# Attention's last group and the first quantised layer: halves, score banks and the causal corner

## The chip, the cores and the metric

The kernel runs on one NeuronCore of a Trainium2 chip. The metric is the device time of one execution, in microseconds (us). The core has five engines with queues of their own: TensorE (PE in the profile, its weight loads PEld), VectorE (DVE), ScalarE (ACT), GpSimd (POOL) and SyncE (SP, which issues the DMAs here). They meet at semaphores only.

## The reference, cut to what matters

A batch of 16 sequences of 1024 rows and 256 channels goes through four residual layers: causal attention with 16 heads of 16 channels, a linear layer on values quantised to a 6-bit grid in blocks of 32, a Mamba block followed by an MLP, and the quantised layer again.

```python
x = x + _L0_attn_a_ref(_layernorm(x, axis=-1), L0_attn_a_Wqkv, L0_attn_a_Wproj)
x = x + _L0_ffn_ref(_layernorm(x, axis=-1), L0_ffn_weight, L0_ffn_bias)
x = x + _L0_attn_b_ref(_layernorm(x, axis=-1), ...)      # Mamba, then MLP
x = x + _L0_ffn_ref(_layernorm(x, axis=-1), L0_ffn_weight, L0_ffn_bias)
...
# in attention
scores = jnp.where(causal, scores, jnp.finfo(scores.dtype).min)
attn = jax.nn.softmax(scores, axis=-1)
y = jnp.einsum('bhqk,bhkd->bhqd', attn, V)
...
# in the quantised layer
scales = jnp.maximum(jnp.max(jnp.abs(blocks), axis=-1) / FP6_E2M3_MAX, eps)
q = _nearest_on_grid(blocks / scales[..., None], _GRID)
```

## The kernel before

A loop (`nc.Fori`, line 1317) makes 16 passes, one for each sequence, each about 655 us. In a pass each engine works through its own program (`sync_program`, `pool_program`, `scalar_program`, `vector_program`, `tensor_program`). The order of work on an engine is written out by hand. Rows stand on the 128 partitions, in 8 tiles of 128 rows; a half is 4 tiles (512 rows), a pair is 2.

**Attention** runs on one unit counter `u` that all engines' programs share. The 16 heads form 4 groups of 4. For each group come 48 S units: one score product for the row maxima (PE lines 1108, 1111 with the mask), reduced by DVE (line 836). One group and 14 units later come the group's 48 T units: a transposed score product (line 1132; on the diagonal a second product adds `mask2`, line 1135), whose exponential ACT writes to `PT` (line 619). Four T units (the four heads) form a step: one tile of 128 keys against up to 512 queries. The widths of the steps of a group are 512, 384, 256, 128 (first half of queries, all on the diagonal) and 512 x 4, 512, 384, 256, 128 (second half, the last four on the diagonal); steps count from 0 to 47 over the pass. Each step has four value products (line 1145), one step behind the exponentials (`pv_at`), summed in bank 6 until the half's last step. Then ACT evacuates bank 6 (line 626), PE transposes into bank 7 (line 1156), and DVE divides into `Y` (lines 859, 860). A T product waits until the exponential that used its PSUM bank is done: three banks, and from T unit 132 (`T6`), behind the last S unit, six.

**Behind attention** DVE's program runs in this order: `add_tiles(0, U)` adds the projected rows (line 793) and collects statistics (726, 732, 734); `quant_half(0, 0, th)` for the two halves normalises (738) and rounds to the grid (lines 240 to 262, two pairs side by side); `add_tiles(1, X)`; `layer_norm(1, th)` for both halves; `rms_rows(0, th)` for both (826). GpSimd computes the reciprocal roots (511, 517, 518), adds the bias (522) and multiplies the scales back (527). PE turns pairs of tiles (`turn`, line 1070), ACT evacuates them to `XNT` (601), PE multiplies tile by tile (`rows`, line 1087, two banks of rotation or more). Behind that the Mamba block starts with in-projections (PE line 1168, ACT line 647).

Of the kernel before, what the change touches and what calls it, by code (L numbers as in the profile page):

```python
# [76 lines left out]
def build(nc, x_in, wqkv_in, wproj_in, ipw_in, convw_in, convb_in, xpw_in, dtw_in, dtb_in, alog_in, d_in, opw_in,  # L77
          w1_in, w2_in, fw_in, fb_in, ident_in, mask_in, sel_in, cos_in, sin_in, ones_in, out):
    with ExitStack() as ctx:
# [17 lines left out]
        mask2 = sb("mask2", [P, P], BF16)  # L97
# [39 lines left out]
        PT = view(20480, 4096).rearrange("p (s t) -> p s t", s=2 * HG)  # L137
# [126 lines left out]
        with nc.Block() as block:  # L264
# [15 lines left out]
            def _(dve):  # L280
# [4 lines left out]
                nc.vector.tensor_copy(mask2[:, :], mst[:, 1, :])  # L285
# [18 lines left out]
            def _(pe):  # L304
                pe.wait_ge(pre["pool"], 1)

                for i in range(2):
# [22 lines left out]
        pv_at = [STEP_AT + HG * (s + 1) for s in range(NST * NG)]  # L330
# [49 lines left out]
        def row_bank(stage, i):  # L380

            return i % MB if stage == 2 else i % (2 * MB)
# [123 lines left out]
        def pool_program(pool):  # L506
# [13 lines left out]
            def quantized(f, k, th):  # L520
# [3 lines left out]
                  .then_inc(S("xb"), 1)  # L524
                for p in range(th * NT // 4, (th + 1) * NT // 4):
# [44 lines left out]
            quantized(1, 2, 0)  # L570
            layer_power(2, 1)
            quantized(1, 2, 1)
# [20 lines left out]
        def scalar_program(act):  # L593
            own = Chain(act, S("act_own"))

            def evacuate(rnd, pairs=range(NT // 2)):

                for p in pairs:
                    n = rnd * (NT // 2) + p
                    act.wait_ge(S("te_ready"), n + 1)  # L600
                    A(XNT[:, :, 2 * P * p:2 * P * (p + 1)], bank(6 + n % 2).rearrange("p (c t) -> p c t", c=NC),  # L601
# [10 lines left out]
            for u in range(U_END):  # L612
                n = u - NS1 - LAG
                if 0 <= n < NS2 * NG:
                    s, hh, g, qc, j, q0, w = t_unit(n)
                    act.wait_ge(S("ST"), n + 1)
                    if s >= 2:
                        act.wait_ge(S("PV"), s - 1)
                    A(PT[:, (s % 2) * HG + hh, 0:w], bank(t_bank(n))[:, 0:w], ACT.Exp, scale=DH ** -0.5)\  # L619
# [7 lines left out]
            evacuate(0)  # L627
# [154 lines left out]
        def vector_program(dve):  # L782
# [19 lines left out]
            def add_tiles(stage, base):  # L802

                for i in range(NT):
                    add_tile(stage, base, i)
                    if i:
                        tile_stats(stage, i - 1)
                tile_stats(stage, NT - 1)
# [250 lines left out]
        def tensor_program(pe):  # L1059

            def turn(rnd, src, after, count, pairs=range(NT // 2)):

                for p in pairs:
                    n = rnd * (NT // 2) + p
                    pe.wait_ge(S(after), count(p))
                    if n >= 2:
                        pe.wait_ge(S("te_done"), n - 1)
                    for tt in range(2):
                        for c in range(NC):
                            ins = nc.tensor.transpose(bank(6 + n % 2)[:, (2 * c + tt) * P:(2 * c + tt + 1) * P],  # L1070
# [3 lines left out]
            def rows(stage, weights, lhs, k_tiles, rnd=None, which=range(NT)):  # L1074

                for i in which:
# [6 lines left out]
                    banks = MB if stage == 2 else 2 * MB  # L1083
# [17 lines left out]
            for u in range(U_END):  # L1101
# [20 lines left out]
                if 0 <= n < NS2 * NG:  # L1122
# [253 lines left out]
```

## Time and profile before

| What | Value |
|---|---|
| median of 3 runs | 10632.09 us (10631.8 to 10632.46) |
| the profiled execution | 10632.12 us, span 10630.5 us |
| PE busy | 8101.7 us (76%) |
| DVE busy | 8122.4 us (76%) |
| ACT busy | 4281.5 us (40%) |
| POOL busy | 3406.1 us (32%) |
| TensorE clock, mean granted | 0.888 of 2.4 GHz |

How to read the rows below. A row of stretches gives the stretch's bounds and length in us, then the busy time of PE, PEld, DVE, ACT and POOL with the count of instructions, the granted TensorE clock (1.00 is 2.4 GHz, 0.50 is 1.2 GHz), the DMA share and GB/s. A row of the timeline gives start, duration (us), engine, line, operation, output and input, count, and in brackets how long the engine had been idle and who ended that. Durations of pipelined instructions overlap, so the distance between two starts is the cost of one. A row of a group gives the line, engine, operation, shapes and count, then busy us and the mean ns of one, then idle us before it.

### The profile page before, as it was taken

The numbers are of one execution on the slowest core, as the hardware profiler recorded it, in microseconds if no ns is written. First come the engines' busy times: TensorE is split into PE (matmuls) and PEld (weight loads), VectorE is DVE, ScalarE is ACT, GpSimd is POOL, SyncE is SP. The second block draws the span as 40 slices with busy tenths as digits, with TensorE's granted clock in tenths as the row PEclk, the third lists the DMA queues.
The fourth block names the chain that finished last, engine by engine and source line by source line (L and its number), as shares of the span: only waits on it lengthen the run. The fifth ranks groups of instructions, "written<-read, shape, count | busy, mean of one in ns | idle before, by whom it ended". The sixth has DMA issues, their size and how long they took to land. (4 is left out here: it accounts for less than half of the span.)

```text
span 10630.5 us, 101592 instructions
## 1 busy us (share of the span) xinstructions
PE 8101.7 (76%) x34228; PEld 3995.5 (38%) x34228; DVE 8122.4 (76%) x12583; ACT 4281.5 (40%) x8183; POOL 3406.1 (32%) x1895
## 2 busy tenths in 40 slices
PE   5778787787867877777777778778777787777877
PEld 2343343433434334343343434334343243432434
DVE  5776968779687696877868778687786967869677
ACT  2424434254342533425335253342534435344342
POOL 0340614315043150422505225151240513406134
PEclk8898988889888898888989889898898988989889
DMA  3020020200202002030020300202011020200202
GB/s 72 1 43 6 4 45 0 48 1 8 41 0 48 1 11 38 0 48 1 17 33 0 49 1 20 29 0 49 1 29 21 0 49 1 36 13 4 45 0 48
DMA packets 249261, 230.18 MB, mean 22 GB/s; under 512 B 24006, under 2 KB 208582, under 8 KB 248534
## 3 DMA queue, kind: packets, MB, share of 16 engines
q1 hardware_dynamic: 248732, 223.49, 12.8%
q8 instruction: 288, 4.72, 0.2%
q14 instruction: 241, 1.97, 0.1%
HBM read 151.60 MB, written 70.25 MB: 21 GB/s over the span
## 5 line engine op out<-in xcount | busy, mean ns | idle before, releaser
L557 POOL TENSOR_TENSOR arena<-arena 128x1024 f32<-128x1024 f32 x1024 | 2409.3, 2354 | 2146.3 <-DVE arena L928 879.0
L696 ACT ACTIVATE PS<-arena,Aneg 128x512 f32<-128x512 f32 x2048 | 1413.6, 691 | 2046.5 <-DVE XNT L968 1079.9
L619 ACT ACTIVATE arena<-PS 128x512 f32<-128x512 f32 (+3 forms) x3072 | 1312.7, 501 | 957.6 <-PE PS L1135 800.7
L836 DVE TENSOR_REDUCE pm<-PS 128x1 f32<-128x512 f32 (+3 forms) x2048 | 1138.7, 584 | 577.4 <-PE PS L1111 396.8
L1230 PE MATMUL PS<-arena,sel 96*128 96x512 bf16 x2048 | 656.8, 404 | 1037.4 <-DVE arena L944 549.5
L1108 PE MATMUL PS<-arena 96*128 96x512 bf16 (+3 forms) x3072 | 1114.5, 380 | 370.6 <-PEq L1325 272.1
L511 POOL TENSOR_TENSOR rstd<-ve,mhalf 128x4 f32<-128x4 f32 x96 | 105.1, 1095 | 3168.6 <-DVE ve L734 3168.6
L1242 PE MATMUL PS<-arena,identf 128*128 128x512 f32 x2048 | 1070.6, 649 | 0.0
L1242 PE MATMUL PS<-XNT,identf 128*128 128x512 f32 x2048 | 970.8, 597 | 0.0
L1132 PE MATMUL PS<-arena 99*128 99x512 bf16 (+3 forms) x3072 | 924.3, 330 | 15.5 <-DMA arena<-arena 15.5
L1070 PE MATMUL PS<-identf,arena 128*128 128x128 f32 x1280 | 268.2, 369 | 778.5 <-POOL arena L527 663.4
L1230 PEld LDWEIGHTS PS<-arena,sel 96*128 96x128 bf16 x2048 | 132.6, 98 | 1773.0 <-DVE arena L944 878.7
L601 ACT ACTIVATE XNT<-PS 128x512 f32<-128x512 f32 x320 | 184.1, 597 | 1389.2 <-PE PS L1070 1389.2
L1108 PEld LDWEIGHTS PS<-arena 96*128 96x128 bf16 x3072 | 312.2, 102 | 1035.5 <-DVE pm L836 451.2
L1145 PE MATMUL PS<-arena 128*32 128x512 f32 (+3 forms) x6144 | 653.8, 498 | 21.1 <-ACT arena L626 21.1
L968 DVE TENSOR_TENSOR_SCAN XNT<-PS,hlast,arena 128x512 f32<-128x512 f32 x512 | 626.7, 1263 | 12.3 <-POOL arena L557 12.3
L968 DVE TENSOR_TENSOR_SCAN arena<-PS,arena 128x512 f32<-128x512 f32 x512 | 595.6, 1202 | 52.3 <-POOL arena L557 51.8
L968 DVE TENSOR_TENSOR_SCAN arena<-PS,hlast,arena 128x512 f32<-128x512 f32 x512 | 626.3, 1262 | 1.0 <-POOL arena L557 1.0
L944 DVE TENSOR_TENSOR XNT<-XNT,PS 128x1024 f32<-128x1024 f32 x512 | 610.0, 1191 | 16.7 <-PE PS L1230 16.7
L944 DVE TENSOR_TENSOR arena<-arena,PS 128x1024 f32<-128x1024 f32 x512 | 609.0, 1190 | 0.0
L968 DVE TENSOR_TENSOR_SCAN XNT<-PS,arena 128x512 f32<-128x512 f32 x512 | 595.3, 1201 | 15.6 <-POOL arena L557 15.6
L1242 PEld LDWEIGHTS PS<-arena,identf 128*128 128x128 f32 x2048 | 427.1, 209 | 418.2 <-issue 364.3
(140 smaller groups left out, 13882.6 us busy)
## 6 DMA issues: line engine op xcount, KB each, us to landing
pieces_scratch<-arena SPq DMA_DIRECT2D x272, 192.0 KB, 2.5
arena<-pieces_scratch SPq DMA_DIRECT2D x102, 512.0 KB
arena<-pieces_scratch SPq DMA_DIRECT2D x204, 128.0 KB
arena<-pieces_scratch SPq DMA_DIRECT2D x102, 256.0 KB
arena<-in_x SPq DMA_DIRECT2D x17, 1024.0 KB, 5.6
U<-in_x SPq DMA_DIRECT2D x17, 1024.0 KB, 5.5
out<-X SPq DMA_DIRECT2D x64, 256.0 KB, 18.0
arena<-arena SPq DMA_DIRECT2D x192, 8.0 KB, 1.9
```

Of the source, the lines that this page charges most:

```text
L557: nc.gpsimd.tensor_tensor(DB[:, n % 2], DTU[:, j, half(th)].unsqueeze(1).to_broadcast([P, SP2, TH]), BB[:, SP2 * sg:SP2 * (sg + 1), :], AL ...
L619: A(PT[:, (s % 2) * HG + hh, 0:w], bank(t_bank(n))[:, 0:w], ACT.Exp, scale=DH ** -0.5)\
L696: A(bank(da_bank(m)), DT[:, j, half(th)], ACT.Exp, scale=Aneg[:, j, SP2 * sg + ss:SP2 * sg + ss + 1]).then_inc(S("dA"), 1)
L836: V_.tensor_reduce(out=dst, in_=bank(u % 3)[:, 0:w], op=ALU.max, axis=AX.X, negate=True).then_inc(S("red"), 1)
L944: V_.tensor_tensor(hs, hs, PS[:, c_bank(0):c_bank(0) + SP2, :], ALU.mult)\
L968: V_.tensor_tensor_scan(HS[n % len(HS)][:, ss, :], bank(da_bank(m)), DB[:, n % 2, ss, :], hlast[:, j, s:s + 1] if th else 0.0, ALU.mult, A ...
L1070: ins = nc.tensor.transpose(bank(6 + n % 2)[:, (2 * c + tt) * P:(2 * c + tt + 1) * P], src(p, tt)[:, c * P:(c + 1) * P], identf[:, :])
L1108: ins = MM(bank(u % 3)[:, 0:w], QS[0:SR, h, tile(i)], KS[0:SR, h, c * TH:c * TH + w], start=True, stop=not diag)
L1132: ins = MM(bank(t_bank(n))[:, 0:w], KS[0:SR + PIECES, h, tile(j)], QS[0:SR + PIECES, h, q0:q0 + w], start=True, stop=not diag)
L1145: ins = MM(PS[VW * hh:VW * (hh + 1), 6, TH - w:TH], V[:, j, g * HG + hh, :], PT[:, (s % 2) * HG + hh, 0:w], start=j == 0, stop=s == last_o ...
L1230: ins = MM(bank(c_bank(ss)), sel[:, DS + SP2 * sg + ss, :], BCP[:, half(th)], start=True, stop=True)
L1242: ins = MM(bank(4 + jt % 2), identf[:, :], HS[k % len(HS)][:, ss, :], start=False, stop=sg == NSG - 1 and ss == SP2 - 1)
```

## The change

- `mask2` and its products on PE are gone. After the exponentials of a step on the diagonal, GpSimd's `affine_select` sets the corner of `PT` above the diagonal to zero, for the four heads at once (semaphore `cut`); PE waits for it before the step's value products.
- `PT` has three buffers of four heads instead of two, and the value products come one step later (`pv_at`).
- T products use three banks throughout; `T6` is gone.
- When `y` of the last group's first half is written (`EARLY_AT`), the first half of the projection follows inside the unit loop: two turned pairs at `EARLY_TURN` and two units later (in step 44), and at `EARLY_ROWS` (first unit of step 45) the first four row tiles on PE, and on DVE `add_tiles(0, U, 0)` and `quant_half(0, 0, 0)`. They use banks 0 to 2. GpSimd has the power and the bias add of this half ahead of the cut of step 44.
- Behind attention the halves alternate on DVE, and GpSimd's order follows.
- The first quantised layer's buffers move to where `QS` and `KS` of earlier groups lay.

```diff
-        PT = view(20480, 4096).rearrange("p (s t) -> p s t", s=2 * HG)
+        PT = [view(at, 2048).rearrange("p (s t) -> p s t", s=HG) for at in (20480, 22528, 29696)]
...
-            return view(20480 * f + 2048 * n + 512 * p, 512)
+            if f == 0:
+                return view((0, 2048, 4096, 8192, 10240)[n] + 512 * p, 512)
+            return view(20480 + 2048 * n + 512 * p, 512)
...
-        pv_at = [STEP_AT + HG * (s + 1) for s in range(NST * NG)]
+        pv_at = [STEP_AT + HG * (s + 2) for s in range(NST * NG)]
...
-        T6 = -(-(NU - NS1 - LAG) // 6) * 6
+        DIAG_STEP = [q0 == j * P for _, _, _, _, j, q0, _ in (t_unit(HG * s) for s in range(NST * NG))]
 
         def t_bank(n):
-            return 3 + n % 3 if n < T6 else n % 6
+            return 3 + n % 3
+
+        EARLY_Y = y_at[pv_at[last_of[NTH * (NG - 1)]] + HG + 2]
+        EARLY_AT = pv_at[last_of[EARLY_Y]] + HG + 2
+        EARLY_TURN, EARLY_ROWS = EARLY_AT + 3, EARLY_AT + 7
+
+        def turn_bank(n):
+
+            return 0 if n < NT // 4 else 6 + n % 2
...
         def row_bank(stage, i):
 
+            if stage == 0 and i < NT // NTH:
+                return 1 + i % 2
...
# GpSimd
-            layer_power(0, 0)
+            for s in range(NST * NG):
+                if s == NST * NG - HG:
+                    layer_power(0, 0)
+                    add_bias(0, 0)
+                if DIAG_STEP[s]:
+                    corner = PT[s % len(PT)][:, :, 0:P]
+                    pool.wait_ge(S("expd"), HG * (s + 1))
+                    nc.gpsimd.affine_select(out=corner, in_=corner, pattern=[[0, HG], [1, P]],
+                                            compare_op=ALU.is_ge, fill=0.0, base=0, channel_multiplier=-1)\
+                      .then_inc(S("cut"), 1)
+
+            rescale(0, 0)
             layer_power(0, 1)
-            quantized(0, 0, 0)
-            quantized(0, 0, 1)
+            add_bias(0, 1)
             layer_power(1, 0)
+            rescale(0, 1)
+            rms_power(0, 0)
             layer_power(1, 1)
-            rms_power(0, 0)
             rms_power(0, 1)
...
# ACT
-                    if s >= 2:
-                        act.wait_ge(S("PV"), s - 1)
+                    if s >= len(PT):
+                        act.wait_ge(S("PV"), s - len(PT) + 1)
...
-            evacuate(0)
+                if u in (EARLY_TURN + 1, EARLY_TURN + 3):
+                    evacuate(0, [(u - EARLY_TURN) // 2])
+            evacuate(0, range(NT // 4, NT // 2))
             evacuate(1)
...
# DVE
-            add_tiles(0, U)
-            quant_half(0, 0, 0)
+                if u == EARLY_ROWS:
+                    add_tiles(0, U, 0)
+                    quant_half(0, 0, 0)
+            add_tiles(0, U, 1)
+            dve.wait_ge(S("xb"), 1)
+            add_tiles(1, X, 0)
             quant_half(0, 0, 1)
+            layer_norm(1, 0, lambda i: U[:, i, :])
             dve.wait_ge(S("xb"), NTH)
-            add_tiles(1, X)
-
-            for th in range(NTH):
-                layer_norm(1, th, lambda i: U[:, i, :])
-            for th in range(NTH):
-                rms_rows(0, th)
+            add_tiles(1, X, 1)
+            rms_rows(0, 0)
+            layer_norm(1, 1, lambda i: U[:, i, :])
+            rms_rows(0, 1)
...
# PE
-                    if T6 <= n < T6 + 3:
-                        pe.wait_ge(S("red"), NU)
-                    elif n >= 3:
-                        pe.wait_ge(S("expd"), n - 2 if n < T6 else n - 5)
-                    diag = q0 == j * P
-                    ins = MM(bank(t_bank(n))[:, 0:w], KS[0:SR + PIECES, h, tile(j)],
-                             QS[0:SR + PIECES, h, q0:q0 + w], start=True, stop=not diag)
-                    if diag:
-                        ins = MM(bank(t_bank(n))[:, 0:P], identb[:, :], mask2[:, :], start=False, stop=True)
-                    ins.then_inc(S("ST"), 1)
+                    if n >= 3:
+                        pe.wait_ge(S("expd"), n - 2)
+                    MM(bank(t_bank(n))[:, 0:w], KS[0:SR + PIECES, h, tile(j)],
+                       QS[0:SR + PIECES, h, q0:q0 + w], start=True, stop=True).then_inc(S("ST"), 1)
...
                     pe.wait_ge(S("expd"), HG * (s + 1))
+                    if DIAG_STEP[s]:
+                        pe.wait_ge(S("cut"), sum(DIAG_STEP[:s + 1]))
...
-            turn(0, lambda p, tt: Y[:, 2 * p + tt, :], "y", lambda p: NTH * NG)
-            rows(0, wproj, xt, NC, rnd=0)
+                if u in (EARLY_TURN, EARLY_TURN + 2):
+                    turn(0, lambda p, tt: Y[:, 2 * p + tt, :], "y", lambda p: EARLY_Y + 1, [(u - EARLY_TURN) // 2])
+                if u == EARLY_ROWS:
+                    rows(0, wproj, xt, NC, rnd=0, which=range(NT // NTH))
+            turn(0, lambda p, tt: Y[:, 2 * p + tt, :], "y", lambda p: NTH * NG, range(NT // 4, NT // 2))
+            rows(0, wproj, xt, NC, rnd=0, which=range(NT // NTH, NT))
             quant_products(0)
```

## Rows read from the trace of the kernel before

**Rows 1.** Busy time of each engine in three stretches of one pass

```profile
1492.00:1578.00 86.00, 85.86 (x698) 39.93 (x697) 69.78 (x151) 59.48 (x136) 0.00 (x0) 0.99 0.01 2
1622.00:1634.00 12.00, 0.00 (x0) 0.00 (x0) 11.97 (x25) 0.00 (x0) 3.48 (x3) 0.58 0.00 0
1662.00:1668.00 6.00, 5.36 (x19) 3.89 (x20) 2.27 (x9) 2.39 (x4) 1.32 (x2) 0.50 0.00 0
```

**Rows 2.** Groups of instructions on PE from 1492 to 1578 us

```profile
L1135 PE MATMUL PS<-mask,identb 128*128 128x128 bf16 x83 | 18.4, 222 | 0.0
```

**Rows 3.** Timeline of PE, last group's tail

```profile
1579.25 0.22 PE L1135 MATMUL PS<-mask,identb 128*128 128x128 bf16 x1
1579.31 0.33 PE L1132 MATMUL PS<-arena 99*128 99x384 bf16 x1
...
1597.94 1.07 PE L1145 MATMUL PS<-arena 128*32 128x512 f32 x8
1598.94 1.04 PE L1132 MATMUL PS<-arena 99*128 99x512 bf16 x4
...
1600.90 0.39 PE L1132 MATMUL PS<-arena 99*128 99x512 bf16 x1
```

**Rows 4.** Timeline of ACT, tail and first in-projections

```profile
1595.19 9.98 ACT L619 ACTIVATE arena<-PS 128x512 f32<-128x512 f32 x20
...
1608.32 0.60 ACT L626 ACTIVATE arena<-PS 128x512 f32<-128x512 f32 x1 [0.54 <-PE PS L1145]
...
1670.87 0.60 ACT L647 ACTIVATE arena<-PS 128x512 f32<-128x512 f32 x1 [1.12 <-PE PS L1168]
```

**Rows 5.** Timeline of DVE, from attention's last y to the RMS rows

```profile
1609.96 0.42 DVE L860 TENSOR_TENSOR arena<-PS,rl 128x256 f32<-128x256 f32 x1
1613.89 0.42 DVE L793 TENSOR_TENSOR X<-U,PS 128x256 f32<-128x256 f32 x1 [3.51 <-PE PS L1087]
...
1618.55 0.17 DVE L734 TENSOR_SCALAR ve<-mv 128x4 f32<-128x4 f32 x1
...
1621.55 1.37 DVE L738 TENSOR_SCALAR arena<-X,mv,rstd 128x256 f32<-128x256 f32 x4
...
1634.27 2.83 DVE L738 TENSOR_SCALAR arena<-X,mv,rstd 128x256 f32<-128x256 f32 x4
...
1648.45 0.74 DVE L793 TENSOR_TENSOR X<-X,PS 128x256 f32<-128x256 f32 x2
...
1653.40 0.42 DVE L793 TENSOR_TENSOR X<-X,PS 128x256 f32<-128x256 f32 x1 [2.56 <-PE PS L1087]
...
1658.17 0.17 DVE L734 TENSOR_SCALAR ve<-mv 128x4 f32<-128x4 f32 x1
...
1663.51 1.14 DVE L826 TENSOR_SCALAR arena<-U,rms 128x256 f32<-128x256 f32 x4 [0.39 <-POOL rms L518]
```

**Rows 6.** Timeline of POOL (GpSimd), the same stretch

```profile
1618.80 1.02 POOL L511 TENSOR_TENSOR rstd<-ve,mhalf 128x4 f32<-128x4 f32 x1 [181.23 <-DVE ve L734]
...
1623.00 2.34 POOL L522 TENSOR_TENSOR X<-X,bias 128x1024 f32<-128x1024 f32 x1
1633.82 2.48 POOL L527 TENSOR_TENSOR arena<-arena,sc 128x512 f32<-128x512 f32 x2 [8.48 <-DVE arena L262]
```

**Rows 7.** Groups of instructions by shape, whole execution

```profile
L928 DVE TENSOR_TENSOR arena<-arena 128x512 f32<-128x512 f32 x128 | 188.4, 1472 | 0.5
...
L771 DVE TENSOR_TENSOR arena<-arena 128x512 f32<-128x512 f32 x136 | 94.1, 692 | 4.6
...
L502 POOL TENSOR_SCALAR arena<-arena 128x512 bf16<-128x512 f32 x136 | 84.5, 622 | 813.3 <-DVE arena L778 813.3
```

**Rows 8.** Timeline of PE, transition after attention

```profile
1610.44 1.09 PE L1070 MATMUL PS<-identf,arena 128*128 128x128 f32 x8 [0.81 <-DVE arena L860]
...
1612.83 7.07 PE L1087 MATMUL PS<-wproj,XNT 128*128 128x256 f32 x32
...
1649.49 2.12 PE L1070 MATMUL PS<-identf,arena 128*128 128x128 f32 x8 [6.81 <-POOL arena L527]
```

More of the change, by code:

```diff
@@ L96, in build @@
         mask1 = sb("mask1", [P, P], BF16)
-        mask2 = sb("mask2", [P, P], BF16)
         cosT = sb("cosT", [P, NT, DH])
@@ L284, in _ @@
                 nc.vector.tensor_copy(mask1[:, :], mst[:, 0, :])
-                nc.vector.tensor_copy(mask2[:, :], mst[:, 1, :])
                 nc.vector.tensor_copy(sel[:, :, :], stage[0:3 * 2 * DS])
@@ L349, in t_unit @@
             return s, hh, g, qc, j, q0, (qc + 1) * TH - q0
-        T6 = -(-(NU - NS1 - LAG) // 6) * 6
+        DIAG_STEP = [q0 == j * P for _, _, _, _, j, q0, _ in (t_unit(HG * s) for s in range(NST * NG))]
         def t_bank(n):
-            return 3 + n % 3 if n < T6 else n % 6
+            return 3 + n % 3
+        EARLY_Y = y_at[pv_at[last_of[NTH * (NG - 1)]] + HG + 2]
+        assert EARLY_Y == NTH * (NG - 1)
+        EARLY_AT = pv_at[last_of[EARLY_Y]] + HG + 2
+        EARLY_TURN, EARLY_ROWS = EARLY_AT + 3, EARLY_AT + 7
+        assert EARLY_ROWS + HG < max(y_at) and EARLY_AT > NU
+        def turn_bank(n):
+            return 0 if n < NT // 4 else 6 + n % 2
         NJT = NTH * ND
@@ L518, in rms_power, with add_bias @@
                 nc.gpsimd.tensor_tensor(r, r, mhalf[:, tiles(th)], ALU.pow).then_inc(S("rm"), 1)
-            def quantized(f, k, th):
+            def add_bias(k, th):
                 pool.wait_ge(S("xn"), NT * k + NT // NTH * (th + 1))
@@ L524, in quantized, with rescale @@
                   .then_inc(S("xb"), 1)
+            def rescale(f, th):
                 for p in range(th * NT // 4, (th + 1) * NT // 4):
@@ L569, in pool_program @@
             front_pieces(pool, own, range(NT - 1, NT))
-            quantized(1, 2, 0)
+            add_bias(2, 0)
+            rescale(1, 0)
             layer_power(2, 1)
-            quantized(1, 2, 1)
+            add_bias(2, 1)
+            rescale(1, 1)
         A = nc.scalar.activation
@@ L600, in evacuate @@
                     act.wait_ge(S("te_ready"), n + 1)
-                    A(XNT[:, :, 2 * P * p:2 * P * (p + 1)], bank(6 + n % 2).rearrange("p (c t) -> p c t", c=NC),
+                    A(XNT[:, :, 2 * P * p:2 * P * (p + 1)], bank(turn_bank(n)).rearrange("p (c t) -> p c t", c=NC),
                       ACT.Copy).then_inc(S("te_done"), 1)
@@ L616, in scalar_program @@
                     act.wait_ge(S("ST"), n + 1)
-                    if s >= 2:
-                        act.wait_ge(S("PV"), s - 1)
-                    A(PT[:, (s % 2) * HG + hh, 0:w], bank(t_bank(n))[:, 0:w], ACT.Exp, scale=DH ** -0.5)\
+                    if s >= len(PT):
+                        act.wait_ge(S("PV"), s - len(PT) + 1)
+                    A(PT[s % len(PT)][:, hh, 0:w], bank(t_bank(n))[:, 0:w], ACT.Exp, scale=DH ** -0.5)\
                         .then_inc(S("expd"), 1)
@@ L800, in tile_stats, with add_tiles @@
                     variance(own, tiles(i * NTH // NT), "var")
-            def add_tiles(stage, base):
-                for i in range(NT):
+            def add_tiles(stage, base, th):
+                for i in range(NT)[tiles(th)]:
                     add_tile(stage, base, i)
-                    if i:
+                    if i % (NT // NTH):
                         tile_stats(stage, i - 1)
-                tile_stats(stage, NT - 1)
+                tile_stats(stage, (th + 1) * NT // NTH - 1)
             def grid(f, pairs):
@@ L1067, in turn @@
                         pe.wait_ge(S("te_done"), n - 1)
+                    if n == 1:
+                        pe.wait_ge(S("te_done"), n)
                     for tt in range(2):
                         for c in range(NC):
-                            ins = nc.tensor.transpose(bank(6 + n % 2)[:, (2 * c + tt) * P:(2 * c + tt + 1) * P],
+                            ins = nc.tensor.transpose(bank(turn_bank(n))[:, (2 * c + tt) * P:(2 * c + tt + 1) * P],
                                                       src(p, tt)[:, c * P:(c + 1) * P], identf[:, :])
@@ L1082, in rows @@
                         pe.wait_ge(S("v_done"), NT)
-                    banks = MB if stage == 2 else 2 * MB
+                    banks = MB if stage == 2 else 2 if stage == 0 and i < NT // NTH else 2 * MB
                     if i >= banks:
@@ L1145, in tensor_program @@
                         ins = MM(PS[VW * hh:VW * (hh + 1), 6, TH - w:TH], V[:, j, g * HG + hh, :],
-                                 PT[:, (s % 2) * HG + hh, 0:w], start=j == 0, stop=s == last_of[oc])
+                                 PT[s % len(PT)][:, hh, 0:w], start=j == 0, stop=s == last_of[oc])
                     ins.then_inc(S("PV"), 1)
```

2 rows, old and new, of the table names are left out of this document.

## The prediction

> **What bounds the kernel now.** I read the stretches of one pass of the batch loop first (the pass from 1462 us on; the 16 passes are alike, so 1 us per pass is 16 us of the time). From 1492 to 1578 us, where the score products S of a later head group run beside the exponentials and value products of an earlier one, PE is busy 85.86 of 86 us at full clock, DVE 69.78 [rows 1]: PE is the bound, and an instruction taken from it there shortens the pass. In the last group's tail, PE and ACT work almost in step: 20 exponentials of 512 columns in 9.98 us, 0.5 us each [rows 4], and PE needs 1.96 us for a full step, 1.00 for the value products and 0.96 for four T products (1597.94, 1598.94 and 1600.90: 2.96 us hold two value steps and one of T) [rows 3]. DVE stands idle there. Then comes the transition, 1610 to 1665 us, where DVE is the bound: 11.97 busy of 12 us between 1622 and 1634, PE at nothing and its clock falling to half [rows 1]. The timeline of DVE shows the order: y of the last group at 1609.96, first residual add at 1613.89 (3.51 us of waiting for PE), variance of half 0 at 1618.55, normalise at 1621.55, behind it the grid until 1634.27, the same for half 1 until 1648.45, a wait of 2.56 us for PE at 1653.40, the last variance at 1658.17, the last RMS rows at 1663.51 [rows 5]. The change aims at both stretches.
>
> **Part 1, the mask products go.** In 1492 to 1578 stand 83 of them [rows 2]; each delays the next product by 0.06 us (1579.25 to 1579.31) [rows 3]. 83 x 0.057 is 4.7 us. DVE has 16 us of slack in those 86, but in steps with narrow T tiles it is close behind PE, so I take 4.0 us; the ends are 3.0 and 4.7. The other 45 or so lie in the tail or ahead and are in part 3. One DVE copy at the start goes too: nothing.
>
> **Part 2, GpSimd cuts the corner.** 32 new instructions per pass, 4 x 128 elements on 128 partitions, and PE waits for each before that step's value products. No such instruction is in the trace. Nearest rows: a one-input GpSimd operation on 512 elements, 622 ns [rows 7]; from above the 1024-element bias add, 2.34 us [rows 6]. I take 1.0 us, because it has one input and 512 elements. Below nothing isn't possible, it is added work on an engine that idles there. In the main stretch it is hidden: value products now follow two steps (over 4 us) behind the exponentials, and the PT buffers are three, so ACT waits for the same value product as before. Behind PE's wait stand S and T products, which matter only if a cut takes longer than a step.
>
> **Part 3, the tail with three banks.** Before, the last 60 T products had six banks; now three. T product n waits for exponential n-3, so the fourth of a step waits for the first exponential of its step: 0.60 (exponential, as an evacuation of its size [rows 4]) + 0.05 (semaphore, estimated) + 0.31 (product and weight switch) + 1.00 (value products) + 0.42 (next product until ACT starts) = 2.38 us per full step, against 1.96. By the same sum with each step's own widths, or ACT's time where that is longer, and 0.5 for an evacuation and 0.5 for the output transposes: steps 33 to 43 take 2.1, 1.9, 1.9, 2.0, 2.1, 2.4, 1.7, 2.0, 2.5, 2.9, 2.4, together 23.8 us. Before it is 1579.09 to 1600.90, 21.8 [rows 3]. So +2.0 us. The wait for the maxima's DMA lies in the third step in both.
>
> **Part 4, work put into the tail.** Count from the first T product of step 44 (1600.90 before). PE now also does two transposed pairs (0.5 us each) [rows 8], and 4 of the 8 row tiles, 3.5 us of the 7.07 [rows 8]. With the waits for ACT's evacuations between them: pair at 0.3, pair at 2.4, value products to 4.2, rows from 4.35 to 7.9. DVE's first add is 1.06 later than the rows' start (as 1612.83 to 1613.89), at 5.4; the variance comes at 9.5, the power takes 1.02 [rows 6], normalise 1.37 [rows 5], the grid 11.35 (1634.27 less 1622.92): it ends at 23.4. y of the last group stands behind that in DVE's order: it ends at 24.1 instead of 9.48.
>
> GpSimd's queue is the trap here. Ahead of the cut of step 44 stand the power and the bias add (2.34 us), which wait for DVE's normalise. So that cut can't start before 14.5; PE, which is through its other work at 10.3, waits 5 us for it, with the last T products behind it. The last output transposes are done at 16.4 + 4 cuts = 20.4, or near 23 if PE's clock has dropped: still under DVE's 23.4. So the stall is hidden as long as a cut is under 1.75 us.
>
> Three cuts now run beside DVE's grid. In the trace, the four normalisations of half 1 take 2.83 us beside GpSimd's rescale, those of half 0 1.37 without [rows 5, 6]; a DVE add of two SBUF inputs takes 1472 ns on average in the scan stage, where GpSimd runs, and its like 692 elsewhere [rows 7]. So I add 1.5 us (0 to 2.5): y ends at 25.6. The Trainium skill (GPSIMD Engine Reference, "Specifications") says that GpSimd shares its SBUF interfaces with VectorE and contends with instructions of two SBUF inputs or in a two-port mode; the trace agrees, 2.83 against 1.37 us. By that rule the reverse holds too: the normalise of half 1 is now free of it, which I have counted.
>
> **Part 5, what stands behind y.** From the end of y: turn of two pairs and rows of half 1. PE has been idle, and after such a gap its clock is half, 1.2 instead of 2.4 GHz (0.50 in the 6 us from 1662, 0.58 in 1622 to 1634 [rows 1]). A turn of 8 transposes then takes 2.12 us instead of 1.09 [rows 8]. By the pattern from 1649.49 on, the first add comes 4.0 after the start and the variance 8.9 after it [rows 5, 8]. Stage 1 half 0 (turn 1.0, evacuation, rows 3.5 at full clock) has its variance at 13.5; normalise 1.4 and grid 11.4 end at 26.3. Then a normalise hides in the wait for PE, the first add of half 1 comes 4.95 after the grid (1648.45 to 1653.40 before), the last variance 9.9 after it (its row ends at 1658.34): 36.2. RMS rows of half 0 are hidden; power, normalise, squares, two small GpSimd steps and rows of half 1 make 6.1: last row at 42.3. Before, this took 54.3 (the ends of the rows at 1609.96 and 1663.51) [rows 5]. So 12.0 us are gained, not the 17 us of DVE work that was moved: each half now waits for PE alone, where before the other half covered it.
>
> Then turn, and two in-projections until ACT's second copy: 6.2 before (1670.87) [rows 4]. Now only half of the turn is left: 4.1 if the clock is full, 6.7 if it has dropped. I take the middle, 5.4.
>
> **The sum per pass.** From step 44: 25.6 + 42.3 + 5.4 = 73.3, before 69.97 (1600.90 to 1670.87): +3.3. Tail +2.0. Masks -4.0. Together +1.3 us, 16 times: +21 us. The profiled run's time, 10632.12, is the median's (10632.09), its span 10630.5. Forecast: 10653 us. The measurement tells 0.2% (21 us, 1.33 us per pass) from no change, so the likeliest time is on that edge.
>
> **Rivals.** (1) *Faster: the clock holds.* If PE's sparse work between 8 and 23 us keeps its clock up, part 5's first rows take 2.4 us less, the in-projections 1.3 less; with the masks' full 4.7 and no contention the sum is 1.3 - 2.4 - 1.3 - 0.7 - 1.5 = -4.6; of it I expect some 60%: -2.6 us, 10590. For it: value products and transposes lie in that stretch; in the 12 us from 1622, with PE wholly idle, the mean is 0.58, not 0.50, so the clock outlasts some idleness [rows 1]. Against: the waits of 5 and 4 us in it are as long. Chance 0.27. (2) *Slower: a slow cut.* One mechanism: four cuts stand in a row behind the bias add. Above 1.75 us each they, not the grid, set y. At 2.34 us [rows 6] that is +2.4, half clock for the value products in between +0.7, more contention 1.4: 1.3 + 4.5 = 5.8 us, 10725. Against it: the one-input row of 622 ns. The Trainium skill (GPSIMD Engine Reference, "Elementwise — side-by-side cycle accounting") gives 768 ns for 512 elements in the best loop and about 12 cycles an element for data-dependent branches, by which it would be an estimated 5 us. No row here shows which. Chance 0.13. (3) *A wash.* One of the two clock questions goes well, or part 1 gives 4.7: -1.3 to -2.4 from the sum, about 10630. Chance 0.20. (4) *It doesn't do what it says:* the early half starts with three steps left, so little of the idle time is used; that is in the forecast, whose chance is 0.40.
>
> **How the numbers follow.** Forecast 0.40, of which 0.30 lies above 0.2% and 0.10 within. Wash 0.20: 0.17 within, 0.03 faster. Faster 0.27, slow cut 0.13. So faster 0.30, same 0.27, slower 0.43. The range: from 10585 (rival 1's time, -3 us per pass) to 10730 (rival 2's).
>
> **What would show it.** T products with 2.4 us per full step in the tail; no L1135 row and the main stretch 3 to 5 us shorter; a cut near 1 us; an idle PE of about 5 us ended by GpSimd in step 46; the last y some 25 us after step 44 began, directly behind a grid; from y to the last RMS row 42 us; windows at half clock right behind y. The prediction is wrong if PE does not drop its clock there, if cuts cost over 1.75 us, or if the main stretch shrinks by less than 3 us.

## The result: 0.6% slower, and where the time went

| What | Kernel before | Changed kernel |
|---|---|---|
| median | 10631.94 us (10629.89 to 10632.46) | 10692.26 us (10690.29 to 10694.26) |
| profiled execution, span | 10632.12 us, 10630.5 us | 10690.52 us, 10688.9 us |
| TensorE clock, mean granted | 0.888 | 0.885 |

The ratio is 1.0057, 95% interval 1.004 to 1.0075: slower. The totals of the changed kernel's page show what was taken and added: PE 8056.1 us busy (before 8101.7), POOL 3740.9 (before 3406.1), and the 512 cuts of 16 passes at 680 ns. The columns of a group are line, engine, operation, shapes and count, then busy us and mean ns of one, then the idle time before it.

```profile
PE 8056.1 (75%) x32180; PEld 3857.9 (36%) x32180; DVE 8145.8 (76%) x12582; ACT 4262.3 (40%) x8183; POOL 3740.9 (35%) x2407
...
L554 POOL TENSOR_SCALAR_AFFINE_SELECT arena<-arena 128x512 f32<-128x512 f32 x512 | 347.0, 680 | 2202.3 <-ACT arena L646 2202.3
```

To see where the 58 us between the two profiled spans lie I took the starts of the same named instructions in all 16 passes and averaged the distances. T 0, T 132 and T 176 are T products by their unit (T 176 is the first of step 44); y is the last group's last `y` on DVE; the RMS row is the last of half 1; the copy is ACT's second of the in-projections. Us per pass:

| Stretch | Before | Changed | Difference |
|---|---|---|---|
| T 0 to T 132 | 87.38 | 83.35 | -4.03 |
| T 132 to T 176 (steps 33 to 43) | 21.63 | 23.55 | +1.92 |
| T 176 to last y | 9.06 | 25.17 | +16.11 |
| last y to last RMS row | 54.08 | 42.45 | -11.63 |
| last RMS row to second copy | 6.43 | 6.66 | +0.23 |
| Mamba up to its scans | 52.63 | 52.75 | +0.12 |
| scans | 239.13 | 239.54 | +0.41 |
| end of the MLP to the next pass's first S product | 89.00 | 89.45 | +0.45 |

The stretches not listed are equal to 0.01 us. The sum is +3.6 us per pass, 57 us in 16 passes; another 0.9 us lies ahead of the first pass. The stretches vary from pass to pass within one execution too: last y to last RMS row takes 53.31 to 54.42 us before, 41.53 to 43.12 in the changed kernel.

The timeline of PE in the changed kernel, third pass, answers to [rows 3, 8] (start, duration, engine, line, operation, count; in brackets how long the engine had been idle and who ended that):

```profile
1606.06 0.81 PE L1163 MATMUL PS<-arena 99*128 99x512 bf16 x3
1607.13 0.39 PE L1163 MATMUL PS<-arena 99*128 99x512 bf16 x1 [0.26 <-ACT arena L646]
1607.44 1.07 PE L1175 MATMUL PS<-arena 128*32 128x512 f32 x8
...
1612.70 3.62 PE L1121 MATMUL PS<-wproj,XNT 128*128 128x256 f32 x16
...
1623.75 1.93 PE L1175 MATMUL PS<-arena 128*32 128x512 f32 x8 [4.97 <-POOL arena L554]
...
1634.10 1.97 PE L1104 MATMUL PS<-identf,arena 128*128 128x128 f32 x8 [3.44 <-DVE arena L889]
1635.90 5.60 PE L1121 MATMUL PS<-wproj,XNT 128*128 128x256 f32 x16
1641.34 1.04 PE L1104 MATMUL PS<-identf,arena 128*128 128x128 f32 x8
...
1661.75 2.17 PE L1104 MATMUL PS<-identf,arena 128*128 128x128 f32 x8 [15.40 <-POOL arena L541]
```

The fourth T product of a step now waits 0.26 us for an exponential. The early rows stand at 1612.70. Behind them PE idles 4.97 us, and what ends that is a cut. The rows of half 1 take 5.60 us at 1635.90, where 16 of the same kind took 3.62 at 1612.70. GpSimd's timeline tells why the cut is late, DVE's what the cuts do to the grid:

```profile
1618.14 1.02 POOL L523 TENSOR_TENSOR rstd<-ve,mhalf 128x4 f32<-128x4 f32 x1 [19.09 <-DVE ve L763]
1620.66 2.34 POOL L534 TENSOR_TENSOR X<-X,bias 128x1024 f32<-128x1024 f32 x1 [1.50 <-DVE arena L767]
1622.95 2.73 POOL L554 TENSOR_SCALAR_AFFINE_SELECT arena<-arena 128x512 f32<-128x512 f32 x3
1626.94 1.12 POOL L554 TENSOR_SCALAR_AFFINE_SELECT arena<-arena 128x512 f32<-128x512 f32 x1 [1.26 <-ACT arena L646]
```

```profile
1613.77 0.42 DVE L822 TENSOR_TENSOR X<-U,PS 128x256 f32<-128x256 f32 x1 [6.80 <-PE PS L1121]
...
1617.89 0.17 DVE L763 TENSOR_SCALAR ve<-mv 128x4 f32<-128x4 f32 x1
...
1621.81 1.30 DVE L243 TENSOR_SCALAR sc<-am 128x16 f32<-128x16 f32 x2
...
1623.35 1.84 DVE L245 TENSOR_TENSOR arena<-arena,rs 128x512 f32<-128x512 f32 x2
1625.11 1.19 DVE L248 TENSOR_SCALAR arena<-arena 128x512 uint32<-128x512 uint32 x2
...
1626.89 1.71 DVE L253 SCALAR_TENSOR_TENSOR arena<-arena 128x512 f32<-128x512 f32 x2
...
1633.62 0.42 DVE L889 TENSOR_TENSOR arena<-PS,rl 128x256 f32<-128x256 f32 x1
1638.02 0.42 DVE L822 TENSOR_TENSOR X<-U,PS 128x256 f32<-128x256 f32 x1 [3.97 <-PE PS L1121]
...
1652.14 1.29 DVE L245 TENSOR_TENSOR arena<-arena,rs 128x512 f32<-128x512 f32 x2
...
1660.71 2.83 DVE L767 TENSOR_SCALAR U<-X,mv,rstd 128x256 f32<-128x256 f32 x4
1666.10 0.42 DVE L822 TENSOR_TENSOR X<-X,PS 128x256 f32<-128x256 f32 x1 [2.55 <-PE PS L1121]
...
1675.44 1.14 DVE L855 TENSOR_SCALAR arena<-U,rms 128x256 f32<-128x256 f32 x4 [2.18 <-POOL rms L530]
```

The last y stands at 1633.62, directly behind the grid; its inputs on PE were done at 1630.66 (1630.00 and 0.66). The waits for PE that follow, 3.97 and 2.55 us, answer to the 3.51 and 2.56 of [rows 5]. Added up over all residual adds between the last y and the last RMS row, DVE waits 10.1 us per pass for PE, where it waited 7.0 before: each half waits for PE alone. ACT's second copy starts at 1682.92, 6.3 us after the last RMS row's end. The table of stretches (start:end, length, busy time and count of PE, PEld, DVE, ACT, POOL, granted clock, DMA share, GB/s):

```profile
1501.00:1584.00 83.00, 82.09 (x612) 34.46 (x614) 70.75 (x152) 58.23 (x136) 12.75 (x20) 0.99 0.01 2
...
1624.00:1634.00 10.00, 5.78 (x40) 1.75 (x32) 9.97 (x18) 1.49 (x5) 3.90 (x4) 0.67 0.00 0
1634.00:1640.00 6.00, 5.90 (x18) 4.92 (x19) 0.74 (x3) 1.19 (x2) 1.33 (x2) 0.52 0.01 3
1640.00:1648.00 8.00, 6.10 (x31) 4.87 (x30) 6.35 (x26) 1.08 (x2) 1.03 (x1) 1.00 0.00 1
```

In the main stretch PE is still full (82.09 of 83 us), so taking products from it paid. Right behind the last y, where everything waits for PE, its clock is 0.52, that is 1.2 GHz.

### The profile page after: what moved, and what is told of

It reads as the page before. It is cut to its first block and busy times, and to the rows that moved or that the text cites. A ratio compares the mean times of both kernels' runs of the same rounds, so it can differ in the third digit from the quotient of the medians.

```text
span 10688.9 us, 98472 instructions
## 1 busy us (share of the span) xinstructions
PE 8056.1 (75%) x32180; PEld 3857.9 (36%) x32180; DVE 8145.8 (76%) x12582; ACT 4262.3 (40%) x8183; POOL 3740.9 (35%) x2407
## 3 DMA queue, kind: packets, MB, share of 16 engines
q14 instruction: 241, 1.97, 0.1%
## 5 line engine op out<-in xcount | busy, mean ns | idle before, releaser
L554 POOL TENSOR_SCALAR_AFFINE_SELECT arena<-arena 128x512 f32<-128x512 f32 x512 | 347.0, 680 | 2202.3 <-ACT arena L646 2202.3
L1175 PE MATMUL PS<-arena 128*32 128x512 f32 (+3 forms) x6144 | 681.9, 522 | 79.5 <-POOL arena L554 79.5
L1000 DVE TENSOR_TENSOR_SCAN arena<-PS,arena 128x512 f32<-128x512 f32 x512 | 595.7, 1202 | 52.4 <-POOL arena L582 51.8
```

What stands on the lines that cost most here:

```text
L554: nc.gpsimd.affine_select(out=corner, in_=corner, pattern=[[0, HG], [1, P]], compare_op=ALU.is_ge, fill=0.0, base=0, channel_multiplier=-1)\
L1000: V_.tensor_tensor_scan(HS[n % len(HS)][:, ss, :], bank(da_bank(m)), DB[:, n % 2, ss, :], hlast[:, j, s:s + 1] if th else 0.0, ALU.mult, A ...
L1175: ins = MM(PS[VW * hh:VW * (hh + 1), 6, TH - w:TH], V[:, j, g * HG + hh, :], PT[s % len(PT)][:, hh, 0:w], start=j == 0, stop=s == last_of[oc])
```

## The experiments

All ratios are to the kernel before, run beside each variant on the same chip. Its median was 10615.84 us beside cut_only, three_banks, pool_order and y_first, 10625.11 beside alternate_only, double_cut, clock_kept and six_y_first, and 10634.84 beside six_banks and six_y_clock, so ratios are compared, not times. The stretches come from one profiled execution of each kernel, and that of the kernel before took 10632.12 us. So the sum of stretches and the ratio can differ by some 1 us per pass: cut_only has -3.2 by its stretches and -2.2 by its medians, three_banks +3.2 and +4.4. Stretches in us per pass:

| Kernel | Ratio (95%) | T 0 to 132 | to T 176 | to y | to RMS row | to copy |
|---|---|---|---|---|---|---|
| before | 1 | 87.38 | 21.63 | 9.06 | 54.08 | 6.43 |
| changed | 1.0057 (1.004, 1.0075) | 83.35 | 23.55 | 25.17 | 42.45 | 6.66 |
| cut_only | 0.9966 (0.9954, 0.9979) | 83.18 | 20.60 | 9.27 | 54.71 | 6.42 |
| three_banks | 1.0066 (1.005, 1.0083) | 87.45 | 24.33 | 10.13 | 54.02 | 6.40 |
| alternate_only | 1.0107 (1.0091, 1.0124) | 87.36 | 21.65 | 9.06 | 59.87 | 6.74 |
| six_banks | 1.0008 (0.9999, 1.0018) | 83.25 | 20.74 | 25.17 | 41.96 | 6.57 |
| pool_order | 1.007 (1.0053, 1.0087) | 83.36 | 23.64 | 24.77 | 42.24 | 6.62 |
| double_cut | 1.0074 (1.0057, 1.0091) | 83.32 | 23.74 | 26.92 | 41.35 | 6.47 |
| clock_kept | 1.0009 (1.0, 1.0019) | 83.31 | 23.47 | 25.18 | 39.93 | 6.51 |
| y_first | 1.000 (0.999, 1.0009) | 83.28 | 23.64 | 15.51 | 47.49 | 6.54 |
| six_y_first | 0.9887 (0.987, 0.9903) | 83.29 | 20.84 | 15.51 | 42.87 | 6.41 |
| six_y_clock | 0.9812 (0.9795, 0.9828) | 83.58 | 20.83 | 15.51 | 42.42 | 4.53 |

My theory (A) was the prediction's own sum: masks pay, three banks and the early half cost. The rival (B) put the loss on PE's wait for the cut that is queued behind the bias add.

### The cut alone (cut_only)

The kernel before with the cut instead of the mask products, three `PT` buffers and value products one step later; six banks, no early half, old order.

```diff
+                if DIAG_STEP[s]:
+                    nc.gpsimd.affine_select(...)            # mask2 and its products are gone
-        pv_at = [STEP_AT + HG * (s + 1) for s in range(NST * NG)]
+        pv_at = [STEP_AT + HG * (s + 2) for s in range(NST * NG)]
```

> The kernel before with the mask products replaced by GpSimd's cut alone: three PT buffers, value products one step later, six banks in the tail and the old order behind attention kept. Theory A (the loss of the changed kernel comes from the early half: DVE's grid stands ahead of the last y, and each half then waits for PE alone): the main stretch shrinks by 4.0 us per pass, the tail by up to 1, the last cut costs 1: -3.5 to -5.5 us per pass, 10545 to 10575 us. Theory B (the cut itself, through PE's wait for GpSimd, is what costs): 10632 or more.

Measured: 10581.06 us, ratio 0.9966 (0.9954 to 0.9979), faster, but by 2.2 us per pass (3.2 by the stretches) and not by the 3.5 to 5.5 that were expected. The main stretch loses 4.20 us, steps 33 to 43 another 1.03; 1.2 us of that are given back from the MLP's end to the next pass and 0.6 in the transition, which were not edited. The period goes from 654.95 to 651.80. A cut takes 635 ns, and PE's value products wait 4.6 us for cuts in all 16 passes together, by the groups of its waits. So the mask part holds in its own stretch as the prediction had it; the expectation for the whole was missed because stretches that were not edited grew, for a cause that no run shows.

### The banks alone (three_banks), and taken back (six_banks)

```diff
-            return 3 + n % 3 if n < T6 else n % 6
+            return 3 + n % 3
```

> The kernel before with three score banks in the tail too, nothing else. The prediction's sum has +2.0 us per pass for steps 33 to 43 (with the masks gone there); with the steps behind it and the masks kept I expect +2 to +3.5: 10664 to 10688 us. If ACT's backlog covered the handshake it would be 10632.

Measured: 10686.2 us, ratio 1.0066: +2.70 us to T 176 and +1.07 to y. By the ratio the total is above what was expected (1.0030 to 1.0053 of the 10632 us that it was stated on), by the stretches it is inside. To T 176 it takes 24.33 us where the changed kernel, without the masks, takes 23.55. Its PE timeline shows the step of 2.39 us (1610.76 to 1613.15), with the same 0.26 us wait:

```profile
1610.76 0.39 PE L1130 MATMUL PS<-arena 99*128 99x512 bf16 x1 [0.26 <-ACT arena L619]
...
1613.15 0.39 PE L1130 MATMUL PS<-arena 99*128 99x512 bf16 x1 [0.26 <-ACT arena L619]
```

six_banks is the changed kernel with six banks from T 132 to T 173, and three again from where the early half needs banks 0 to 2:

```diff
-            return 3 + n % 3
+            return n % 6 if T6 <= n < T6 + 42 else 3 + n % 3
```

> The changed kernel with six score banks kept from T product 132 to 173, three only from there, where the early half needs banks 0 to 2. If the three banks are a term of their own, steps 33 to 43 fall from 23.6 to about 20.7 us and everything behind stays: -2.8 us per pass, 0.9957 of the changed kernel, about 1.0015 of before. If the tail's time only moves into a later wait, the stretch from T176 to the last y grows by as much and the time stays at 1.0057 to 1.007.

Measured: 10643.04 us, ratio 1.0008 (0.9999 to 1.0018). Steps 33 to 43 take 20.74 instead of 23.55 us; from T 176 to y nothing changes. The banks are worth 2.8 us per pass in the changed kernel, 45 of its 60 us by this stretch and 52 by the ratios. The early half never needed only three banks in those steps.

### The alternating order alone (alternate_only)

The kernel before with the changed kernel's order on DVE and GpSimd behind attention, nothing early.

```diff
-            add_tiles(0, U)
+            add_tiles(0, U, 0)
             quant_half(0, 0, 0)
-            quant_half(0, 0, 1)
-            dve.wait_ge(S("xb"), NTH)
-            add_tiles(1, X)
+            add_tiles(0, U, 1)
+            dve.wait_ge(S("xb"), 1)
+            add_tiles(1, X, 0)
+            quant_half(0, 0, 1)
```

> The kernel before with nothing but the order behind attention changed to the alternating one (DVE and GpSimd); no early half, masks, six banks and two PT buffers kept. Theory A (each half now waits alone for PE and for GpSimd's power, nothing covers it): from the last y to the last RMS row 61 us instead of 54, so +7 us per pass, +112 us, about 1.0105 of before. Rival: alternating is free and only the work put into attention's tail costs: within 0.002 of before.

Measured: 10743.51 us, ratio 1.0107; last y to last RMS row 59.87 us, 5.8 more than before (expected some 7). The rival, alternation for nothing, falls. Another 0.9 us is in the scans, which were not edited. The grid of half 1 now stands behind the second layer's adds of half 0, and these wait for PE with no grid left to cover it. DVE's timeline:

```profile
1652.80 0.42 DVE L799 TENSOR_TENSOR X<-X,PS 128x256 f32<-128x256 f32 x1 [1.68 <-PE PS L1095]
1654.43 0.42 DVE L799 TENSOR_TENSOR X<-X,PS 128x256 f32<-128x256 f32 x1 [1.22 <-PE PS L1095]
...
1675.82 0.42 DVE L799 TENSOR_TENSOR X<-X,PS 128x256 f32<-128x256 f32 x1 [2.12 <-PE PS L1095]
```

So alternation has no gain of its own. No run has the early half with the old order behind it, so whether alternation pays once half 0's grid is out of the way is not shown.

### PE's wait for the cut (pool_order, double_cut)

pool_order puts the cut of step 44 ahead of the power and the three other cuts ahead of the bias add; nothing else differs from the changed kernel.

```diff
-                if s == NST * NG - HG:
+                if s == NST * NG - HG + 1:
                     layer_power(0, 0)
-                    add_bias(0, 0)
...
+            add_bias(0, 0)
             rescale(0, 0)
```

> The changed kernel with GpSimd's order mended: the cut of step 44 ahead of the power, all other cuts ahead of the bias add. PE's wait of 5 us in step 46 must go. Theory A (DVE's grid sets the last y): y comes earlier only by what the cuts slowed the grid, 1.3 us; 10665 to 10680 us. Theory B (PE's stall behind GpSimd sets it): -5 us per pass, about 10612 us.

Measured: 10689.91 us, ratio 1.007. The wait of 4.97 us is gone (PE's output transposes end at 1621.02 and it then waits 10.07 us for y), and y comes 0.40 us earlier, no more: theory B falls. Theory A's size was missed as well, 1.3 us and 10665 to 10680 us were expected, and the total is no shorter than the changed kernel's. What is left of the contention has only moved. First GpSimd's timeline, then DVE's:

```profile
1616.52 1.27 POOL L553 TENSOR_SCALAR_AFFINE_SELECT arena<-arena 128x512 f32<-128x512 f32 x2
...
1619.05 2.34 POOL L534 TENSOR_TENSOR X<-X,bias 128x1024 f32<-128x1024 f32 x1
```

```profile
1616.59 2.00 DVE L767 TENSOR_SCALAR arena<-X,mv,rstd 128x256 f32<-128x256 f32 x4 [1.14 <-POOL rstd L523]
...
1619.82 1.68 DVE L243 TENSOR_SCALAR sc<-am 128x16 f32<-128x16 f32 x2
```

The four normalisations take 2.00 us beside two cuts, where they take 1.38 alone, and line 243 takes 1.68, where it took 1.30 in the changed kernel: together 1.0 us of contention instead of 1.42 (1.84, 1.19 and 1.71 instead of 1.29, 0.75 and 1.28).

double_cut does the cut twice, the second time on zeros.

```diff
+                    own.link(nc.gpsimd.affine_select(...))   # the same corner
                     nc.gpsimd.affine_select(...).then_inc(S("cut"), 1)
```

> The changed kernel with every cut done twice, one behind the other. A cut of 0.64 us becomes 1.4. The prediction's bound says that a cut is hidden under 1.75 us: the stretch T0 to T132 unchanged within 0.2 us, y later only by contention with the grid, up to 2 us per pass: 1.006 to 1.010 of before. If PE's wait for GpSimd is on the path: 4 more cuts behind the bias add are +3 us per pass on top, over 1.010.

Measured: 10704.97 us, ratio 1.0074 (1.0057 to 1.0091). The main stretch is untouched, 83.32 us with 32 more GpSimd instructions: the value products' extra step of delay hides a cut twice as long. y comes 1.75 us later, though PE's wait is only 1 us longer; DVE's grid, which lies beside four more cuts, sets it: its lines 248, 250 and 253 take 1.62, 1.62 and 2.15 us (1.19, 0.75 and 1.71 in the changed kernel), and it ends at 1637.5, when PE's transposes have been done since 1634.13. 1.1 us come back behind y, since PE worked later and its rows ran at a better clock (4.47 us for the 16 of half 1 instead of 5.60): from T 176 to the copy the stretches sum to 74.28 in the changed kernel and to 74.74 here.

```profile
1627.19 1.94 PE L1177 MATMUL PS<-arena 128*32 128x512 f32 x8 [6.01 <-POOL arena L556]
```

### TensorE's clock behind y (clock_kept)

The changed kernel plus idle products: 20 ahead of the value products of step 44, which wait for the early adds, and 24 ahead of the second turn; they write a free bank that nobody reads. They are added work, and nothing is left out.

```diff
+                    if s == NST * NG - HG:
+                        pe.wait_ge(S("x1"), NT // NTH)
+                        for d in range(20):
+                            MM(bank(1), sel[:, 0, :], sel[:, 4:8, :], start=True, stop=True)
...
+            for d in range(24):
+                MM(bank(1), sel[:, 0, :], sel[:, 4:8, :], start=True, stop=True)
```

> The changed kernel with 44 idle products (bf16, 512 columns, into an unused bank, results overwritten) while PE waits: 20 in front of the cut's wait in step 46, 24 in front of the turn behind the last y. If PE's half clock behind y costs what the sum says, the stretch from y to the last RMS row goes from 42.5 to about 40 us: -2.5 us per pass, 0.996 of the changed kernel, 1.002 to 1.003 of before. If the clock is no part of the loss, it stays at 42.5 and at 1.0057 to 1.007 of before.

Measured: 10636.97 us, ratio 1.0009 (1.0 to 1.0019), against the changed kernel's 1.0057 and the 1.002 to 1.003 that were expected. Last y to last RMS row takes 39.93 us instead of 42.45 (expected about 40), with y where it was (25.18). Its stretches:

```profile
1622.00:1628.00 6.00, 5.02 (x42) 2.42 (x43) 6.00 (x11) 1.27 (x5) 1.29 (x2) 1.00 0.01 3
1628.00:1631.00 3.00, 2.80 (x14) 1.13 (x13) 2.79 (x6) 0.00 (x0) 1.31 (x1) 1.00 0.00 0
1631.00:1640.00 9.00, 8.50 (x46) 7.23 (x47) 4.79 (x17) 2.17 (x4) 2.14 (x3) 1.00 0.00 1
```

The clock stays at 1.00 where the changed kernel had 0.67 and 0.52, so the dropped clock costs 2.5 us per pass there, shown by an edit that changes only that. It was not held in the in-projections, and the copy comes at 6.51 us (6.66 in the changed kernel).

### y ahead of the grid (y_first, six_y_first)

y_first is pool_order with DVE's order changed: only adds and normalise of half 0 stand early; the grid comes behind the last y, where DVE would wait for PE.

```diff
                 if u == EARLY_ROWS:
                     add_tiles(0, U, 0)
-                    quant_half(0, 0, 0)
+                    layer_norm(0, 0, ...)
+            dve.wait_ge(S("xn"), NT // NTH)
+            grid(0, range(0, NT // 4))
             add_tiles(0, U, 1)
+            quant_half(0, 0, 1)
             dve.wait_ge(S("xb"), 1)
             add_tiles(1, X, 0)
-            quant_half(0, 0, 1)
```

> As pool_order, and on DVE the grid of half 0 comes behind the last y instead of ahead of it; half 1's residual adds and grid follow, then the adds of stage 1 half 0. Theory A: y at 16 us behind step 44's start instead of 25.6, PE's rows of half 1 hidden under the grid, last RMS row at 61 instead of 68: -7 us per pass against the changed kernel, about 10575 us. If only DVE's total work counted (theory C: the moved work is what it is, order is nothing) it would stay within 1 us per pass of pool_order.

Measured: 10619.43 us, ratio 1.000 (0.999 to 1.0009), a miss: y at 15.51 as expected, but 47.49 us from there on instead of 45. The cause is in GpSimd's timeline:

```profile
1630.24 2.35 POOL L534 TENSOR_TENSOR X<-X,bias 128x1024 f32<-128x1024 f32 x1 [1.50 <-DVE arena L767]
1644.93 1.02 POOL L523 TENSOR_TENSOR rstd<-ve,mhalf 128x4 f32<-128x4 f32 x1 [12.34 <-DVE ve L763]
1645.92 2.10 POOL L541 TENSOR_TENSOR arena<-arena,sc 128x512 f32<-128x512 f32 x2
```

The rescale of half 1 (line 541) had its input when the grid ended at 1641.5, but the power of layer 1 stands ahead of it and waits for a later variance: 4.4 us lost to the order of a queue. Theory C, order is nothing, falls all the same: from T 176 to the copy the stretches sum to 69.54 us against 73.63 in pool_order. six_y_first swaps those two and takes the six banks back as in six_banks:

```diff
-            layer_power(1, 0)
             rescale(0, 1)
+            layer_power(1, 0)
             rms_power(0, 0)
```

> y_first with two things mended: six score banks again until T product 174, and GpSimd rescales half 1 before it takes the power of stage 1 (in y_first that rescale waited 4.4 us behind it). Expected: steps 33 to 43 in 20.6 us as in cut_only (23.6 in y_first), y to the last RMS row 44 instead of 47.5: -6 us per pass against y_first, about 0.991 to 0.993 of before, faster than cut_only (0.9966) too.

Measured: 10509.32 us, ratio 0.9887 (0.987 to 0.9903), faster than the kernel before by 116 us on the same chip, 0.8% below cut_only by the ratios, and below the 0.991 to 0.993 that were expected. The banks give 2.8 us in steps 33 to 43. Last y to last RMS row is 4.6 us shorter (47.49 to 42.87), and what ends GpSimd's idle time ahead of the rescale is now the grid's last line. No run has the swap alone; in six_banks the banks moved this stretch by 0.5, so the swap's share is some 4.1 to 4.6 us, an estimate.

### The same with idle products (six_y_clock)

six_y_first plus 24 and 60 idle products ahead of the first quantised layer's two turns, and 8 and 14 ahead of the RMS rows' turns, where PE also waits for the second layer's first adds of half 1.

> six_y_first with idle products (as in clock_kept) wherever PE waits behind the last y: 24 and 60 in front of the turns of the quantised halves, 8 and 14 in front of those of the RMS rows. If the half clock still costs there, the stretch from the last y to the last RMS row falls from 42.9 to about 40.5 us and ACT's second in-projection copy follows 5.2 us behind instead of 6.4: -2 to -4 us per pass, 0.983 to 0.986 of before. If DVE covers it all: 0.9887 again.

Measured: 10436.72 us, ratio 0.9812 (0.9795 to 0.9828), the fastest of all and below the 0.983 to 0.986 that were expected. Two of the sizes were wrong, though: y to RMS row lost 0.45 us instead of 2.4, the copy came at 4.53 instead of 6.41 (expected 5.2). The clock is full from y on,

```profile
1600.00:1612.00 12.00, 10.75 (x54) 6.51 (x53) 10.75 (x32) 1.19 (x2) 5.54 (x4) 1.00 0.00 1
```

but in this order DVE's grids cover PE's slow rows: DVE is busy 10.75 of the 12 us. In six_y_first the waits for PE that were left there are short (0.48 and 0.53 us in the third pass). Eight of its 16 passes have none and take 42.4 to 42.5 us from y to the last RMS row; those with such waits take up to 43.8. In six_y_clock all 16 take 42.4 and have none. In this stretch a full clock is worth what the waits for PE are, and no more. Another 2.2 us fell away in the scans (0.8) and between the MLP's end and the next pass (1.4), which I can't attribute.

## Why the prediction was right in sign and 39 us short

The forecast was 10653 us within 10585 to 10730, with slower the likeliest sign; measured were 10692. The range reached up to 10730 only for rival 2's slow cut, which did not come; that 10692 lies inside it is luck in part. By its own steps:

- **Masks:** -4.0 was taken, -4.03 measured; cut_only confirms it alone (-4.20). Right.
- **Price of a cut:** 1.0 us was taken from the one-input row of 622 ns. It is 0.64 us alone and 0.91 to 1.12 beside DVE's grid. The size was off, the hiding was not. Rival 2 (over 1.75 us) is out, and double_cut shows that in the main stretch even 1.3 us are hidden. Of the two figures of the Trainium skill (GPSIMD Engine Reference, "Elementwise — side-by-side cycle accounting") that rival 2 quotes, 768 ns is nearer than the estimated 5 us of data-dependent branches, and both are above the measured 0.64 us.
- **Tail with three banks:** +2.0 was taken, +1.92 measured; 2.38 us per full step, 2.39 in the trace (1610.76 to 1613.15 in three_banks).
- **T 176 to y:** 25.6 was predicted for y's end, measured 25.17 + 0.42 = 25.59. The wait of 5 us for the cut is there (4.97) and hidden, as pool_order shows. Contention was put at 1.5 and is 1.42.
- **y to last RMS row:** 42.3 against 42.45 (starts; the ends differ by under 0.1). That half clock stands behind y was right, and clock_kept prices it at 2.5 us (2.4 was taken).
- **In-projections:** the step that failed. I took 5.4, the middle between 4.1 at full and 6.7 at half clock. Measured from the end of the last RMS row (0.35 us behind its start) are 6.3: the clock was down, 0.69 in the 6 us from 1677, and the turn took 1.97 us, near the 2.12 of half clock. The rows [rows 1] already had 0.50 in the 6 us from 1662, and nothing in the change put work on PE there. 0.9 us per pass. six_y_clock shows the other end, 4.53 - 0.35 = 4.2 us with a full clock.

```profile
1676.11 1.97 PE L1104 MATMUL PS<-identf,arena 128*128 128x128 f32 x8 [3.63 <-DVE arena L855]
...
1677.00:1683.00 6.00, 6.00 (x15) 3.17 (x14) 0.00 (x0) 1.87 (x4) 0.00 (x0) 0.69 0.00 0
```

- **The baseline:** 69.97 us from T 176 to the copy were read from one pass; the mean over 16 is 69.57. 0.4 us.
- **What stood in no term:** +0.12 in Mamba, +0.41 in the scans, +0.45 between the MLP's end and the next pass: 1.0 us. The Mamba part is spread: 14 of the 16 passes before take the 52.75 us of the changed kernel, two take 51.8 and 51.7. In the scans 240.05 us come in four passes of the changed kernel, and 240.19 in one before. The last stretch takes 87.6 to 89.8 us by pass before and 87.3 to 90.7 in the changed kernel, and kernels that differ in nothing there have means of 88.5 to 90.3; SyncE's transfers of the results set its end (the page of the profile has 19.0 us to landing for `out<-X`, 18.0 before; in the third pass the last is issued by 2112.4, and the next pass's first S product starts at 2131.2). For these two it stays open whether they are an effect of the change or spread.

Together 0.9 + 0.1 + 0.4 + 1.0 - 0.1 (tail, masks) = 2.3 us per pass between the predicted +1.3 and the measured +3.6.

Rival 1 (clock holds) would not have reached its 10590 us by the clock alone: with the clock held behind y, clock_kept stands at 1.0009, and the 1.9 us per pass that six_y_clock gained at the in-projections would bring that to an estimated 0.998. Rival 3 (a wash) needed one of the two questions on the clock to go well, or 4.7 us from the masks, and neither came. Rival 4 is out in part, since the early half does run, but its point was right: the work fits the idle time of DVE and not that of the chain. From T 176 on the kernel has 4.7 us more than before (74.28 against 69.57), though 17 us of DVE work were moved ahead: y, which PE waits for, stood behind that work. The prediction saw this and priced it, but didn't see that the order had a better neighbour (y_first with the rescale first): 64.8 us (15.51 + 42.87 + 6.41).

## What to carry to other kernels

Work pulled into an engine's idle time belongs behind the instruction that another engine waits for next, not ahead of it; look for the same inversion in every in-order queue that the moved work passes, because two lines swapped on GpSimd were worth some 4.1 to 4.6 us per pass here (an estimate, since they were swapped together with another edit) and three banks too few 2.8. A change in several parts is best priced part by part: this one held a part worth -4.0 us, hidden under two that cost more. When TensorE has idled ahead of work that others wait for, take the clock of that place from the rows as they are, not the middle of two cases.

## What the runs showed of the hardware

- `affine_select` on 128 x 512 f32 takes 0.64 us on GpSimd, like a plain one-input operation of its size (622 ns in [rows 7]). I had left room up to 2.34.
- A VectorE instruction can stand still until a GpSimd one ends, even a very small one: the two operations of line 243 on 16 elements take 0.29 us in y_first without GpSimd, and 1.30 in the changed kernel, where they end at 1623.1, with the bias add (1620.66 + 2.34 = 1623.0). The reduction of line 241 beside the same bias add kept its 1.28.

```profile
1615.24 0.29 DVE L243 TENSOR_SCALAR sc<-am 128x16 f32<-128x16 f32 x2
```

  The Trainium skill (SBUF — State Buffer, "SBUF: two separate sides") calls the shared ports an exclusive lock that is held for a whole instruction, the loser blocking fully; the trace agrees in this row.
- Products whose results nobody reads can shorten a kernel: 44 of them per pass, some 0.22 us each, took 2.5 us from the transition in clock_kept, and in six_y_clock the 22 ahead of the RMS rows' turns took 1.9 from the step to the in-projections.
